# Rotary angles by TensorE: positions transposed, angles as fractions of a turn in fp16 pieces

## The reference

```python
mod = (_silu(c) @ wmod).reshape(4, 6, 1, 128)          # sa, ca, ga, sb, cb, gb
h = _layernorm(x) * (1 + ca) + sa
q, k, v = h @ wq, h @ wk, h @ wv                        # k, v repeated over 4 heads
logits = h @ wr                                         # [B, 16 heads, T, 4 nodes]
tk_vals, tk_idx = top_k(logits, 2); tk_w = softmax(tk_vals)
member = one_hot(tk_idx, 4).sum(-2) > 0
pos = cumsum(member, axis=2) - member                   # a position for each head, token, node
for n in range(4):
    cos, sin = cos_cache[pos[..., n]], sin_cache[pos[..., n]]   # angle = pos * inv_freq, 32 of them
    qr = q * cos + _rotate_half(q) * sin                # and kr alike
    scores = where(causal & member[..., n][:, :, None, :], (qr @ kr.T) * SCALE, -1e9)
    outs.append(softmax(scores) @ v)
x = x + ga * ((tk_w * outs gathered by tk_idx).sum() @ wo)
h = _layernorm(x) * (1 + cb) + sb
x = x + gb * (top-1 expert of 7, chosen by a router, + shared SwiGLU expert)(h)
```

## Time and profile before

| | us | share of the span |
|---|---|---|
| median of three runs (985.09 to 986.34) | 985.75 | |
| span of the profiled execution | 969.8 | 100% |
| TensorE busy | 842.9 | 87% |
| VectorE busy | 804.5 | 83% |
| ScalarE busy | 749.7 | 77% |
| GpSimd busy | 654.2 | 67% |

### The profile page before, as it was taken

One profiled execution on the slowest core, in us unless ns is written; L12 is line 12 of the kernel. 1 busy time (PEld: TensorE's weight loads), 2 busy tenths in 40 slices (PEclk: granted clock), 3 DMA queues, 4 the chain that ended last, 5 costly groups with the idle time before them and its releaser, 6 DMA issues.

```text
span 969.8 us, 20257 instructions
## 1 busy us (share of the span) xinstructions
PE 842.9 (87%) x6280; PEld 591.5 (61%) x6280; DVE 804.5 (83%) x1854; ACT 749.7 (77%) x2031; POOL 654.2 (67%) x927
## 2 busy tenths in 40 slices
PE   4228979998999899989998999899989999999793
PEld 4225656666666666666566666665666666575693
DVE  4979978997989699969996999699968777777895
ACT  7327797789878887898788878987898887866572
POOL 4257777886887587868885778688856665226493
PEclk9659999999999899999999999999999999999997
DMA  9000000000000000001000100010000000322453
GB/s 210 28 0 8 1 23 24 24 25 24 24 24 24 24 24 25 24 18 30 24 24 18 30 24 24 13 35 24 20 2 2 3 2 3 120 66 84 131 164 118
DMA packets 54282, 36.69 MB, mean 38 GB/s; under 512 B 8384, under 2 KB 53056, under 8 KB 54176
## 3 DMA queue, kind: packets, MB, share of 16 engines
q1 hardware_dynamic: 52960, 32.88, 12.5%
q0 software_dynamic: 1216, 2.51, 0.8%
HBM read 22.23 MB, written 12.36 MB: 36 GB/s over the span
## 4 chain that ended last, share of the span: by engine, by line
PE 56%; DVE 28%; ACT 8%; issue 5%; POOL 2%; DMA 1%; DVEq 0%; ACTq 0%; POOLq 0%; SPq 0%
PE psum L1288 20%; PE psum L1213 8%; PE psum L1313 7%; PE psum L1302 6%; DVE pcs L929 5%; DVE accs L975 4%; DVE psum L964 4%; ACT probs L641 4%; PE psum L1273 3%; PE psum L1293 3%; PE psum L1338 3%; DVE arena L902 2%; DVE negmax L957 2%; PE psum L1275 2%; PE psum L1290 1%
## 5 line engine op out<-in xcount | busy, mean ns | idle before, releaser
L1288 PE MATMUL psum<-QK 128*128 128x128 f32 (+3 forms) x1024 | 383.6, 460 | 1.5 <-ACT QK L620 1.5
L641 ACT ACTIVATE probs<-psum,negmax 128x128 f32<-128x128 f32 (+3 forms) x512 | 266.6, 527 | 78.6 <-DVE negmax L964 46.5
L432 POOL TENSOR_TENSOR R<-pcs 128x512 f32<-128x512 f32 x128 | 190.7, 1511 | 65.6 <-DVE pcs L929 48.0
L964 DVE CUSTOM_DVE_ANT_0 psum<-psum,causal 128x384 f32<-128x384 f32 (+1 forms) x256 | 156.3, 636 | 59.8 <-PE psum L1293 59.8
L1288 PEld LDWEIGHTS psum<-QK 128*128 128x128 f32 x1024 | 168.7, 197 | 46.9 <-issue 41.4
L458 POOL TENSOR_TENSOR coef<-rden,wslot 128x2 f32<-128x2 f32 x256 | 87.7, 342 | 160.0 <-DVE rden L970 159.9
L975 DVE SCALAR_TENSOR_TENSOR accs<-probs,coef,accs 128x128 f32<-128x128 f32 (+3 forms) x256 | 168.8, 660 | 1.0 <-ACT accs L650 1.0
L650 ACT ACTIVATE accs<-probs,coef 128x128 f32<-128x128 f32 (+3 forms) x256 | 148.1, 578 | 24.3 <-POOL coef L458 19.8
L929 DVE TENSOR_TENSOR pcs<-psum,arena 128x512 f32<-128x512 f32 x256 | 161.6, 672 | 0.0
L1302 PE MATMUL psum<-ident,accs 128*128 128x128 f32 x640 | 117.6, 283 | 47.7 <-ACT QK L620 44.1
L620 ACT ACTIVATE QK<-psum 128x384 f32<-128x384 f32 x256 | 125.9, 492 | 1.3 <-PE psum L1275 1.2
(11 more groups left out here) (226 smaller groups left out, 1465.2 us busy)
## 6 DMA issues: line engine op xcount, KB each, us to landing
weight_halves<-whl SPq DMA_DIRECT2D x48, 128.0 KB, 2.2
arena<-weight_halves SPq DMA_DIRECT2D x22, 256.0 KB, 3.2
arena<-weight_halves SPq DMA_DIRECT2D x7, 512.0 KB, 5.9
wst<-in_L_ffn_w_up_dram SPq DMA_DIRECT2D x14, 128.0 KB, 2.4
wst<-in_L_ffn_w_gate_dram SPq DMA_DIRECT2D x14, 128.0 KB, 2.4
wst<-in_L_ffn_w_down_dram SPq DMA_DIRECT2D x14, 128.0 KB, 2.5
sorted_rows<-arena SPq DMA_DIRECT2D x1, 1430.0 KB, 12.0
QK<-sorted_rows SPq DMA_DIRECT2D x5, 260.0 KB, 3.8
```

What stands on the lines that cost most here:

```text
L432: pool.tensor_tensor(R[u][:, :, :, 0:3:2, half * HALF:(half + 1) * HALF].rearrange("p t e j f -> p (t e) j f"), halves(pc, half), halves(p ...
L641: act.activation((expB if e else expA)[:, k % (4 if e else 3), 0:w], area, ACT.Exp, scale=1.0 if k % TB < 2 else -1.0, bias=negmax[k % 4][ ...
L964: dve.tensor_tensor_reduce(score_area(k, e), score_area(k, e), causal[:, T - w:T], -1.0, 3e38, ALU.add, ALU.min, accum_out=negmax[k % 4][: ...
L1288: pe.matmul(o, QK[:, u, e, rows], QK[:, u, 2, 0:w], start=True, stop=False)
```

## The change

Positions reach the angles another way. VectorE still multiplies the counted positions with the memberships (now in fp16), but no longer reduces them. TensorE turns them, and adds the four nodes on the way (`position_rows`: for each sequence 48 matmuls of 32 rows by 128 columns, the same rows written three times, to output partitions 0, 32 and 64). ScalarE copies the result to `posT`, 96 rows by 512 tokens a sequence, scaled. On VectorE, ahead of the wait for the router's logits, `turn_pieces` makes from the frequencies three fp16 tables, each holding the frequency in pieces as fractions of a turn, laid out block by block. `angles` then multiplies 96 position rows with these tables into one PSUM bank: for 128 tokens, 8 heads and 2 slots all 32 frequencies. Two more matmuls in the middle add and subtract a large constant, which rounds to whole turns, so that what remains is a fraction of a turn; sine and cosine take the factor of 2 pi as their scale. Such a tile exists four times before the loop (heads 0 to 7) and 28 times in it, after the second step of heads n with n % 8 < 4, where it takes a turn of the ring of three PSUM banks. VectorE copies a tile out in the following step (`keep_angles`), and once more with the sign bit cleared (`size_angles`); all the parts of L874 to L902 are gone. Before the loop ScalarE takes the sines straight from PSUM, one a tile, and one cosine of 2048 columns.

Beside this, the frequencies are loaded third in SyncE's queue, the codes of the memberships stand ahead of the angles on VectorE, the ring of masks has two buffers instead of three, and with it the weight pieces start one head earlier.

```diff
-            dve.tensor_reduce(slot[:, :, :], prod[:, :, :, :], AX_X, ALU.add).then_inc(S["slots_w"], 1)
-            def angle_product(j, q):
...
-            def angle_turns(j, q, part):
...
-            first_angles(0)
...
-        RING = 3
+        RING = 2
...
+        def angle_tile(k):
+            n, s = k // TB, k % TB
+            if s == 1 and n % SPAN < TB and n // SPAN + 1 < NH // SPAN:
+                return n // SPAN * TB + n % SPAN
+            return None
...
+            if angle_tile(k) is not None:
+                turns.append(("a", angle_tile(k)))
...
+            sp.dma_start(freq[:, :], inv_freq).then_inc(S["c_in"], 16)
             for b in range(B):
                 sp.dma_start(x1[:, b * TB:(b + 1) * TB, :], x[b].rearrange("(t p) d -> p t d", p=P)
...
+                table(turns_all[:, :, :], g_whole, 0, RED, 1.0)
+                table(turns_off[:, :, 0:RED], g_first, 0, RED, -1.0)
+                table(turns_off[:, :, RED:HALF], g_whole, RED, HALF, -1.0)
+                table(turns_low[:, :, :], g_later, 0, RED, -1.0)
...
+            for i in range(4):
+                keep_mask(i)
+            keep_positions(0)
+            keep_mask(4)
+            keep_mask(5)
+            for t_ in range(TB):
+                act.wait_ge(S["ang_abs"], t_ + 1)
+                act.activation(trig[:, 0, 0, :, t_, :, :].rearrange("p h s f -> p h (s f)"),
...
+            for b in range(1, B):
+                keep_positions(b)
+            trigonometry(0)
...
+            def position_rows(b):
...
+                for tb in range(TB):
+                    for n in range(NODES):
+                        for i in range(3):
+                            mm_ = pe.matmul(dst[i * 2 * COLS:(i + 1) * 2 * COLS, tb * P:(tb + 1) * P],
+                                            prod_cols[:, b * TB + tb, :, n], ident16[:, :],
+                                            start=n == 0, stop=n == NODES - 1)
+                mm_.then_inc(S["row_mm"], 1)
+            def angles(dst, j, t_):
...
+                pe.matmul(high, at, turns_[0], start=True, stop=False)
+                pe.matmul(low, at, turns_[1][:, :, RED:HALF], start=False, stop=False)
+                for i in range(2):
+                    pe.matmul(high, identbig[:, :], whole[:, i:i + 1].unsqueeze(2).to_broadcast([P, COLS, RED]),
+                              start=False, stop=False)
+                pe.matmul(high, at, turns_[1][:, :, 0:RED], start=False, stop=False)
+                return pe.matmul(high, at, turns_[2], start=False, stop=True)
...
                 if k < STEPS:
                     row_max(k)
+                if k >= 1 and angle_tile(k - 1) is not None:
+                    keep_angles(angle_tile(k - 1))
                 if k >= 3:
                     weigh_b(k - 3)
                 if 1 <= k <= STEPS:
                     inverse_sums(k - 1)
+                if k >= 1 and angle_tile(k - 1) is not None:
+                    size_angles(angle_tile(k - 1))
...
                     prob_rows(k - 4)
+                if angle_tile(k) is not None:
+                    a = angle_tile(k)
+                    wait_turn(pe, ("a", a))
+                    angles(turn_bank(("a", a)), a // TB + 1, a % TB).then_inc(S["ang_mm"], 1)
```

More of the change, by code:

```diff
@@ L121, in block_kernel @@
         ktok = [ktoks[:, u, :, :, :] for u in range(2)]
-        kdif = sb("kdif", [P, TB, HD])
-        kcod = sb("kcod", [P, TB, HD])
+        kwork = sb("kwork", [P, 2, TB, HD])
+        kdif, kcod = [kwork[:, i, :, :] for i in range(2)]
         QK = sb("QK", [P, 2, 3, T])
@@ L151, in block_kernel @@
         xn = pcs_flat.rearrange("p (t d) -> p t d", d=DIM)
-        gcol = [t_[:, :, :].rearrange("p t d -> p (t d)")[:, i * P:(i + 1) * P] for t_ in (kdif, kcod) for i in range(2)]
+        kwork_flat = kwork[:, :, :, :].rearrange("p k t d -> p (k t d)")
+        gcol = [kwork_flat[:, i * P:(i + 1) * P] for i in range(4)]
         lg = accs[:, 2:4, :].rearrange("p g t -> p (g t)")
@@ L826, in _ @@
+            turn_pieces()
             dve.wait_ge(S["lg_ev"], 2)
@@ L904, in _ @@
-            dve.wait_ge(S["slots_w"], 1)
-            dve.wait_ge(S["loaded"], 16 * 8)
-            def first_angles(q):
-                angle_product(0, q)
-                for part in range(6):
-                    angle_turns(0, q, part)
-            first_angles(0)
-            dif = prod[:, :, 0, :]
-            dve.tensor_tensor(dif, sA, sB, ALU.subtract).then_inc(S["w_step"], 1)
-            dve.wait_ge(S["w_step"], 1)
-            dve.tensor_tensor(dif, dif, L, ALU.mult).then_inc(S["w_step"], 1)
@@ L917, in _ @@
-            dve.wait_ge(S["w_step"], 2)
-            dve.tensor_reduce(lmax[:, 0, :], dif, AX_X, ALU.add).then_inc(S["w_step"], 1)
-            def products(n, e):
-                dve.wait_ge(S["qk_mm"], n + 1)
-                dve.wait_ge(S["trig_done"], 2 * (n // CH + 1) if n < SPAN else 2 * (n // SPAN + 2))
-                if n >= 1 and e == 0:
-                    dve.wait_ge(S["add_done"], 2 * n)
-                src = psM.rearrange("p (t j f) -> p t j f", t=TB, f=HALF)
-                for i, dst in ((1, pc), (0, ps)):
-                    table = trig[:, n // SPAN % 2, i, n % SPAN, :, e, :]
-                    dve.tensor_tensor(dst[:, :, e, :].rearrange("p t (j f) -> p t j f", f=HALF), src,
-                                      table.unsqueeze(2).to_broadcast([P, TB, 4, HALF]), ALU.mult
-                                      ).then_inc(S["prod_done"], 1)
@@ L933, in _ @@
-            for e in range(2):
-                products(0, e)
             for e, i in ((0, 0), (1, 1)):
@@ L949, in _, with angle_place, over_heads @@
             dve.tensor_scalar(cgap[:, :], cgap[:, :], 11.0, -1.0 / 6.0, ALU.add, ALU.mult).then_inc(S["codes_done"], 1)
-            first_angles(1)
-            for e in range(2):
-                products(1, e)
+            def angle_place(j, t_, i):
+                return trig[:, j % 2, i, :, t_, :, :].rearrange("p h s f -> p h (s f)")
+            def over_heads(b_):
+                return b_[:, :].rearrange("p (h c) -> p h c", h=SPAN)
+            for t_ in range(TB):
+                dve.wait_ge(S["ang_mm"], t_ + 1)
+                y_ = over_heads(bank[(5, 1, 2, 3)[t_]])
+                dve.tensor_scalar(angle_place(0, t_, 1).bitcast(U32), y_.bitcast(U32), 0x7FFFFFFF, None, ALU.bitwise_and).then_inc(S["ang_abs"], 1)
@@ new lines, in size_angles, with products @@
+            def size_angles(a):
+                dve.tensor_scalar(angle_place(a // TB + 1, a % TB, 1).bitcast(U32),
+                                  over_heads(turn_bank(("a", a))).bitcast(U32), 0x7FFFFFFF, None, ALU.bitwise_and
+                                  ).then_inc(S["ang_abs"], 1)
+            def products(n, e):
+                dve.wait_ge(S["qk_mm"], n + 1)
+                dve.wait_ge(S["trig_done"], TB + 1 + 2 * (n // SPAN))
+                if n >= 1 and e == 0:
+                    dve.wait_ge(S["add_done"], 2 * n)
+                src = psM.rearrange("p (t j f) -> p t j f", t=TB, f=HALF)
+                for i, dst in ((1, pc), (0, ps)):
+                    table = trig[:, n // SPAN % 2, i, n % SPAN, :, e, :]
+                    dve.tensor_tensor(dst[:, :, e, :].rearrange("p t (j f) -> p t j f", f=HALF), src,
+                                      table.unsqueeze(2).to_broadcast([P, TB, 4, HALF]), ALU.mult
+                                      ).then_inc(S["prod_done"], 1)
@@ L954, in row_max @@
+            for n in range(2):
+                for e in range(2):
+                    products(n, e)
             def row_max(k):
@@ L988, in residual @@
                                   ).then_inc(S["x1_done"], 1)
-            angle_steps = [(q, part) for q in range(2) for part in range(-1, 6)]
             for k in range(STEPS + 3):
@@ L1247, in _, with mask_rows @@
             project(0)
-            for i, (kind, half) in enumerate(((0, 0), (0, 1), (1, 0), (1, 1), (2, 0), (2, 1))):
+            def mask_rows(i):
+                kind, half = i // 2, i % 2
                 if kind:
```

210 lines of the change are left out of this document (129 added, 81 removed).

## The result

The changed kernel takes 976.97 us, the median of four runs (974.37 to 977.98), against 985.44 for the kernel before; the ratio is 0.9909, with a 95% interval of 0.9892 to 0.9925. On a second chip the ratio was 0.9886 (0.9853 to 0.9919). So it is faster by 8.5 us, where 20.8 were forecast.

A forecast was written before the change was run, and what follows sets the result against it. TensorE sets the loop's pace, with stalls added by VectorE's rotary steps. Span 969.8 less 8.3 (loop), 3.5 (first eight heads) and 9.2 (before the loop) is 948.8, plus 15.95: 965 us, range 953 to 977.

The forecast's parts named there:

- the loop's gain: Attention loop, heads 8 to 55: rotary steps gone from VectorE, angle tiles added on TensorE, together -8.3 us.
- an even head with a tile: Loop, third step: TensorE waits 0.25 us for the bank, head ends 1.04 later, about 0.5 remains after absorbed idle time.
- the odd head: Loop: value matmuls come first, so the bank is free long before; a tile adds 0.79 us.
- The prediction's own sign: Pairs with tiles above 24 us, or TensorE idle ahead of the fourth step's transposes, would prove the forecast wrong.
- My third rival: More comes back in the loop if VectorE and GpSimd slow each other: another 7 us, 958; chance 0.10.
- The removal: Loop: without VectorE's rotary steps, pairs of 24.15, 22.78 and 22.58 us fall to 21.8, before tiles are added.
- The start: Before the loop: new position and angle path brings the first transposes near 59.9 us in place of 69.1, -9.2.
- taken at nothing: VectorE's turn pieces and four tables, 6.4 us, fit its 6.96 us logits wait; any overrun at most some 2.
- the first rival: Position matmuls run one after another (971), or weight loads show and tiles cost 1.1 us, not 0.8 (973); chance 0.18.
- The second (cover only, 995): VectorE's steps were only cover in the loop; earlier pairs keep their times and tiles add: 995, slower; chance 0.07.
- The mask ring and the weight pieces: Two mask buffers and earlier weight pieces cost nothing; without load cover each of 62 heads would pay.
- The carried 15.95: Difference between profiled span 969.8 us and timed median 985.75, carried over unchanged to the forecast.

The follow-up runs named there:

- the steps taken out: Kernel before without VectorE's rotary steps for groups two to seven, later sines made from old values: heads 8 to 55 take 569.1 us in place of 586.0.
- the changed kernel's second trace: Changed kernel profiled again, unchanged, with the experiments; against the kernel before's second trace the start gained 6.8 us, the first eight heads 2.8.
- the first trace of before: First profile of the unchanged kernel before: span 969.8 us, without the pause of some 19 us behind the loop; its second profile has span 985.3.
- the run with the late tables: Changed kernel with three of the four fp16 tables moved on VectorE from ahead of the logits wait to behind the position products: 977.15 us.

## Why the prediction was wrong, step by step

The direction and the mechanism at the front were right; the loop's gain was forecast and is not there. Of the 21.0 us of span 9.2 came. Heads 8 to 55 fell 8.4 short, the start 4.1, and the end is 1.1 longer; the first eight heads gave 1.8 more. In heads 8 to 55 the pairs with tiles are 4.5 longer than reckoned, and 2.3 of the forecast gain was the lower clock of one trace; 0.8 are missing in pairs 8j+6, and 0.7 in the rest.

**The failed step: an even head with a tile.** "the weighting starts at 764.20 and would end near 765.87 behind the first of the two": I moved an instruction by 0.68 and kept its 0.99. That duration was 0.44 of waiting for GpSimd and 0.55 of work; moved, it missed the end of the first addition and waited 1.06 for the second. The even head pays 1.6 and 1.2, not "about 0.5". In the odd head, where I added 0.8, it is 0 and 0.4. With both copies ahead of the weighting the even heads pay 0.6 and 0.4, and the odd ones 0.4 and 0.6. The net is 1.6 a pair against 1.3, 3.6 us over twelve pairs; the other 0.9 of the 4.5 is a bare pair of 21.9 in place of 21.8. Moving the copies or cutting GpSimd's instruction takes 0.5 to 0.6 a pair away and leaves 1.0 to 1.1, so this wait, and not TensorE's columns, is what was left out. The prediction's own sign came true: TensorE stands idle ahead of the transposes of the fourth step, 1.02 in head 16. The Trainium skill (SBUF — State Buffer, Who interferes with whom) has the rule that I did not weigh: an instruction of VectorE with two inputs in SBUF and an instruction of GpSimd that reads SBUF exclude each other, and whichever comes second waits for the whole of the other. The traces agree: the weighting ends 0.55 us after GpSimd's instruction in 61 of 64 cases. My third rival only said "if they slow each other", and went on to treat the row's mean as the instruction's own time.

**The removal.** 24 us forecast for heads 8 to 55, 16.9 measured. The row on which it rests was of the same kind: the absolute value's 2.21, from 570.60, is 1.13 left of GpSimd's additions and 1.08 of work.

```profile
568.78 2.94 POOL L432 TENSOR_TENSOR R<-pcs 128x512 f32<-128x512 f32 x2 [0.60 <-DVE pcs L929]
```

That part was right in its effect, since the wait went with the instruction. But I took the first trace's pairs as given, which held 2.3 us more of the lower clock than the second, and the sine stages as untouched, which lost 2.4 to it.

**The start.** "If it overruns, the excess goes to the path, at most some 2 us since GpSimd is working then": this term, taken at nothing, failed by the same wait for GpSimd. I had priced a table at 0.94, and the four took 9.05, and the position products came at 40.31, 3.9 late. Undisturbed a table takes 0.75.

```profile
40.31 2.48 DVE L951 TENSOR_TENSOR yT<-psum,yT 128x512 f16<-128x512 f32 x4
...
49.21 2.88 PE L1326 MATMUL psum<-ident,yT 128*32 128x128 f16 x144
...
63.97 0.66 PE L1373 MATMUL psum<-ident,R 128*128 128x128 f32 x2
```

Everything behind held to within a few tenths: 144 position matmuls in 2.88 (2.9), products of head 0 at 54.7 (50.5 + 3.9), GpSimd's rotation 6.5, the first transposes at 63.97 (59.9 + 3.9). The thirds run side by side, so the first rival falls in that half; its other half, 1.1 us a tile, falls too, since a tile takes 0.72 (46.26 to 46.97 before the loop). By an estimate with the 2.38 of the Trainium skill (TensorE: Matmul & The Clock Gate, Part 3), which the page gives for 512 columns, the batches would have taken 3.7 us; the trace has 2.88, about a third of the 8.8 that were reckoned for one after another.

**The rivals.** The second (cover only, 995) falls by the steps taken out. The third (more comes back) is wrong for the loop; the 5.3 against 3.5 in the first eight heads are no case for it, since the changed kernel's second trace has 2.8 there. The mask ring and the weight pieces cost nothing visible; no wait of TensorE for a mask shows in the table of waits.

**The carried 15.95.** It did no harm to the difference, since the pause is in both kernels' timed runs, but it was taken for a constant without a row that showed it.

## What to carry to other kernels

A duration read from a row may hold a wait for another engine, here VectorE's for GpSimd. Before an instruction is moved, split its time into what was left of GpSimd's running instruction and a rest; if the rest is constant over many rows, forecast with the rest and the new place. And where a span and the timed runs differ by more than a few us, profile again and find the stretch that differs before carrying the difference over.

## What the runs showed of the hardware that was not expected

While GpSimd sends 16 scattering DMAs of 128 rows, the other engines come nearly to a standstill, after the fifth or sixth in the two traces shown above: ScalarE goes on 8 to 10 us after the work that it waits for by the code has ended, and the tail is 19 us longer than in the one trace without the pause. With the weight loads taken from beside it the tail is 149.8 of 152 us, with half the DMAs 140.9. That the scatter is the cause is made likely by the shorter standstill with half of it, and not shown: the first trace of before sends all 16 without a pause.

From head 8 on, TensorE's clock fell to its lower level, 1.2 GHz, in the loop of the changed kernel only in sine stages, and in the first trace once more in head 61. In each of the six sine stages of heads 8 to 55 TensorE once waits 2.0 us; the clock fell behind this wait in heads 12, 20, 28 and 44 of the first trace, in heads 12, 20, 36 and 52 of the second, and in head 52 alone of the version with both copies ahead of the weighting. These are heads 12 and 13 in the changed kernel and in that version (the clock is the third number from the end; a value below 1.00 is a mean over both levels):

```profile
204.80:235.20 30.40, 27.75 (x176) 19.93 (x173) 17.97 (x46) 25.14 (x62) 18.01 (x31) 0.89 0.07 19
```
```profile
203.20:230.90 27.70, 25.01 (x176) 17.48 (x173) 17.93 (x46) 25.09 (x62) 18.13 (x31) 1.00 0.07 21
```

That is 2.7 us between the two for the same work, and which pairs it hits changes from trace to trace. In the six sine stages together it makes 5.4 us between these two traces, nearly as much as the move of the copies gained in its pairs, and in the run with the late tables it took back part of the start's gain.
